# Cross attention with its queries, keys and values projected in three f16 products

## The reference

```python
x = x + self_attention(layernorm(layernorm(x)))        # 16 heads of 64, causal
x = x + cross_attention(layernorm(x), ctx)              # below
x = x + mixture_of_experts(layernorm(x))                # 8 experts, top 2, capacity

def cross_attention(x, context, w_qkv, w_proj, b_proj):  # 16 heads of 8, per batch
    q, k, v = split(x @ w_qkv.T)                         # 128 x 128 each
    k = concatenate([context_k, k])                      # 128 + 128 keys
    v = concatenate([context_v, v])
    attn = softmax(q * 8 ** -0.5 @ k.T)
    return (attn @ v) @ w_proj.T + b_proj
```

## Time and profile before

| | |
|---|---|
| median of 3 runs | 1158.15 us (1156.07 to 1158.4) |
| profiled execution | 1158.08 us, its span 1156.2 us |
| PE busy | 1074.3 us, 93% |
| DVE, ACT, POOL busy | 830.5, 674.7, 457.6 us |
| mean granted TensorE clock | 0.981 of full speed |
| self-attention alone | to about 435 us |
| cross attention, joined at first | about 439 to 866 us |
| expert weights and experts | about 866 us to the end |

### The profile page before, as it was taken

The page is one execution under the profiler, slowest core; times in us unless marked ns, Lnnn a source line. Parts: engine busy times, 40 slices in busy tenths (PEclk is TensorE's granted clock), DMA queues, the critical chain, the costliest instruction groups (busy, mean ns, idle before and its releaser), DMA issues.

```text
span 1156.2 us, 30982 instructions
## 1 busy us (share of the span) xinstructions
PE 1074.3 (93%) x12235; PEld 800.0 (69%) x12235; DVE 830.5 (72%) x1921; ACT 674.7 (58%) x1510; POOL 457.6 (40%) x799
## 2 busy tenths in 40 slices
PE   5999999999999998989999999999966999999997
PEld 4788888888888886667767677677643666565664
DVE  4776667776667774677777777777737788888887
ACT  2666666666656665555555565565534755555554
POOL 3444444444444444244344354453322522222222
PEclk9999999999999999899999999999976999999999
DMA  7000000000000000000000000002100000000000
GB/s 169 2 2 2 2 2 2 1 2 2 2 1 2 2 1 10 11 11 15 11 15 11 11 16 11 12 16 68 55 1 0 2 10 11 11 10 11 10 11 10
DMA packets 20658, 16.01 MB, mean 14 GB/s; under 512 B 7042, under 2 KB 18596, under 8 KB 20516
## 3 DMA queue, kind: packets, MB, share of 16 engines
q1 hardware_dynamic: 20176, 13.90, 4.6%
q10 hardware_dynamic: 340, 0.14, 0.1%
HBM read 11.94 MB, written 2.10 MB: 12 GB/s over the span
## 4 chain that ended last, share of the span: by engine, by line
PE 64%; issue 18%; DVE 8%; POOL 7%; ACT 2%; DMA 1%; SPq 0%; DVEq 0%; POOLq 0%
PE ps L971 56%; POOL h_lo L500 5%; PE ps L1022 5%; ACT q_shifted L572 2%; PE ps L1183 1%; DVE xT L677 1%; DMA wv<-in_L_attn_W_v 1%; DVE bst L852 1%; DVE x_all L848 1%; POOL probs L385 1%; PE ps L1213 1%; DVE padded L789 1%; DVE mv L855 1%; PE ps L1201 0%; PE ps L979 0%
## 5 line engine op out<-in xcount | busy, mean ns | idle before, releaser
L807 DVE TENSOR_REDUCE nmax<-ps 128x2 f32<-128x512 f32 x256 | 164.7, 686 | 15.4 <-PE ps L971 15.4
L597 ACT ACTIVATE probsT<-ps 128x512 f32<-128x512 f32 x256 | 139.7, 603 | 41.9 <-PE ps L971 41.0
L500 POOL TENSOR_TENSOR h_lo<-wk,h_hi 128x512 f16<-128x512 f32 x64 | 73.9, 1155 | 185.7 <-ACT h_hi L641 182.8
L535 ACT ACTIVATE probs<-ps,nmax 128x128 f32<-128x128 f32 x512 | 143.1, 384 | 6.9 <-DVE nmax L660 6.9
L529 ACT COPY probsT<-ps 128x512 f32<-128x512 f32 x128 | 75.2, 587 | 116.3 <-PE ps L1022 116.3
L385 POOL TENSOR_TENSOR probs<-probs,rinv 128x512 f32<-128x512 f32 x128 | 133.0, 1040 | 15.9 <-DVE rinv L670 15.9
L971 PE MATMUL ps<-probsT,va 128*32 128x128 f32 x2048 | 137.8, 277 | 0.0
L633 ACT ACTIVATE wq<-ps 128x512 f32<-128x512 f32 x128 | 76.6, 598 | 73.7 <-PE ps L971 73.6
L971 PEld LDWEIGHTS ps<-probsT,va 128*32 128x32 f32 x2048 | 103.0, 110 | 17.0 <-issue 6.7
L660 DVE TENSOR_REDUCE nmax<-ps 128x4 f32<-128x512 f32 x128 | 83.5, 673 | 38.9 <-PE ps L971 38.9
L955 DVE TENSOR_TENSOR h_lo<-wk,h_hi 128x512 f16<-128x512 f32 x64 | 71.8, 1122 | 43.8 <-ACT h_hi L641 43.8
(11 more groups left out here) (204 smaller groups left out, 2552.3 us busy)
## 6 DMA issues: line engine op xcount, KB each, us to landing
ctx_row<-in_ctx SPq DMA_DIRECT2D x32, 128.0 KB, 2.0
out_x<-x_all SPq DMA_DIRECT2D x8, 256.0 KB, 2.3
kT<-in_L_ffn_down_proj_w SPq DMA_DIRECT2D x1, 1024.0 KB, 10.8
wq<-in_L_attn_W_q SPq DMA_DIRECT2D x1, 512.0 KB, 5.0
wk<-in_L_attn_W_k SPq DMA_DIRECT2D x1, 512.0 KB, 8.8
wv<-in_L_attn_W_v SPq DMA_DIRECT2D x1, 512.0 KB, 10.4
wo<-in_L_attn_W_o SPq DMA_DIRECT2D x2, 256.0 KB, 6.7
x_all<-in_x SPq DMA_DIRECT2D x1, 256.0 KB, 3.0
```

Source lines behind the costliest of these rows:

```text
L500: nc.gpsimd.tensor_tensor(h_lo[:, e % 2, 0, :], hT[:, 0, :], h_hi[:, e % 2, 0, :], ALU.subtract).then_inc(hidden_low_first, 1)
L535: last = nc.scalar.activation(probs[:, u, i * P:(i + 1) * P], ps[u][:, i * P:(i + 1) * P], ACT.Exp, bias=nmax[:, u, i:i + 1])
L597: last = nc.scalar.activation(probsT[:, 2 * (t % 2) + a, :], ps[2 + a][:, :], ACT.Exp)
L807: last = nc.vector.reduce_max(nmax2[:, b % 2, t:t + 2, l + a], ps[a][:, :].rearrange("p (t k) -> p t k", t=2), AX_X, negate=True)
```

## The change

Cross attention's normalised input and its weights are split in two f16 parts each. The input's high part `xT2_hi` is written by ACT from the transpose's bank with a factor 16, and DVE makes the low part `xT2_lo` from the bank and the high part; both are kept in place of `xT2`. The weights are split once, in `prepare_cross`, with a factor 16 (`w2_hi`, `w2_lo`), and the threefold columns exist in both parts. Each f32 product is now three f16 products into the same place: high by high, low by high, high by low. The factor 256 that the banks then carry is taken out by the readers: `pack` multiplies the bank by 1/256 (a constant) and adds ACT's part, which ACT now makes with the mask as a scale (`q_sub`, `k_sub`); the copy of v has a constant scale.

```diff
+                    if g == 3 and valid(2):
+                        act.wait_ge(ca_xT_in_bank, b + 3)
+                        if valid(-2):
+                            act.wait_ge(ca_output, b - 1)
+                        nc.scalar.activation(xT2_hi[:, :], ps[7][:, 0:P], ACT.Copy, scale=X2_SCALE).then_inc(ca_xT_high, 1)
...
-                        dve.wait_ge(ca_xT_in_bank, n + 1)
-                        if valid(-2):
-                            dve.wait_ge(ca_output, b - 1)
-                        nc.vector.tensor_copy(xT2[:, :], ps[7][:, 0:P]).then_inc(ca_xT_taken, 1)
+                        dve.wait_ge(ca_xT_high, n + 1)
+                        nc.vector.scalar_tensor_tensor(out=xT2_lo[:, :], in0=ps[7][:, 0:P], scalar=X2_SCALE, in1=xT2_hi[:, :],
+                                                       op0=ALU.mult, op1=ALU.subtract).then_inc(ca_xT_taken, 1)
...
-                        nc.scalar.copy(q_hi[:, :, :], ps[5][:, :]).then_inc(ca_q_high, 1)
+                        nc.scalar.activation(q_sub[:, :, :], ps[5][:, :], ACT.Identity,
+                                             scale=low_q[:, 0:1]).then_inc(ca_q_subgh, 1)
...
-                        nc.scalar.activation(k_hi[:, :, :], ps[5][:, :], ACT.Identity,
-                                             bias=k_bias[:, 0:1]).then_inc(ca_k_high, 1)
+                        nc.scalar.activation(k_sub[:, :, :], ps[5][:, :], ACT.Identity, scale=low_k[:, 0:1],
+                                             bias=k_bias[:, 0:1]).then_inc(ca_k_subgh, 1)
...
-            def pack(dst, hi, bank, low):
-
-                return nc.vector.scalar_tensor_tensor(out=dst, in0=hi, scalar=low[:, :], in1=bank,
+            def pack(dst, part, bank):
+
+                return nc.vector.scalar_tensor_tensor(out=dst, in0=bank, scalar=1.0 / QKV_SCALE, in1=part,
                                                       op0=ALU.mult, op1=ALU.add)
...
+                        w_hi2, w_lo2 = (wqR_hi, wqR_lo) if g == 1 else (wkR_hi, wkR_lo)
                         for t in range(4):
-                            last = mm(ps[5][:, t * P:(t + 1) * P],
-                                      (wqR if g == 1 else wkR)[:, t, :, :, :].rearrange("p l a e -> p (l a e)"), xT2[:, :])
+                            for k, (w, xs) in enumerate(((w_hi2, xT2_hi), (w_hi2, xT2_lo), (w_lo2, xT2_hi))):
+                                last = mm(ps[5][:, t * P:(t + 1) * P], w[:, t, :, :, :].rearrange("p l a e -> p (l a e)"),
+                                          xs[:, :], k == 0, k == 2)
...
-                        mm(ps[6 if valid(0) else 4][:, 0:P], xT2[:, :], wqkvT[:, 2, :]).then_inc(ca_v_in_bank, 1)
+                        for k, (xs, w) in enumerate(((xT2_hi, w2_hi), (xT2_hi, w2_lo), (xT2_lo, w2_hi))):
+                            last = mm(ps[6 if valid(0) else 4][:, 0:P], xs[:, :], w[:, 2, :], k == 0, k == 2)
+                        last.then_inc(ca_v_in_bank, 1)
```

More of the change, by code:

```diff
@@ L36 @@
 SHIFT = 16.0
+X2_SCALE = 16.0
+W2_SCALE = 16.0
+QKV_SCALE = X2_SCALE * W2_SCALE
 KEYS2 = 2 * P
@@ L171, in build @@
         xT_lo = sb("xT_lo", [P, P], F16)
-        wqR = sb("wqR", [P, 4, 4, 4, E2])
-        wkR = sb("wkR", [P, 4, 4, 4, E2])
+        wqR_hi = sb("wqR_hi", [P, 4, 4, 4, E2], F16)
+        wqR_lo = sb("wqR_lo", [P, 4, 4, 4, E2], F16)
+        wkR_hi = sb("wkR_hi", [P, 4, 4, 4, E2], F16)
+        wkR_lo = sb("wkR_lo", [P, 4, 4, 4, E2], F16)
+        w2_hi = sb("w2_hi", [P, 3, P], F16)
+        w2_lo = sb("w2_lo", [P, 3, P], F16)
         k_bias = sb("k_bias", [P, 1])
         keys4 = sb("keys4", [P, H, 4, E2], F16)
-        q_hi = sb("q_hi", [P, 4, P], F16)
-        k_hi = sb("k_hi", [P, 4, P], F16)
+        q_sub = sb("q_sub", [P, 4, P], F16)
+        k_sub = sb("k_sub", [P, 4, P], F16)
         q_part = sb("q_part", [P, 2, 4, P], F16)
@@ L191, in build @@
         xn2 = sb("xn2", [P, D])
-        xT2 = sb("xT2", [P, P])
+        xT2_hi = sb("xT2_hi", [P, P], F16)
+        xT2_lo = sb("xT2_lo", [P, P], F16)
         xn3 = sb("xn3", [P, D])
@@ L601, in cross_attention @@
                         act.wait_ge(ca_v_in_bank, n + 1)
-                        nc.scalar.copy(va[:, n % 3, 1, :, 0:E2], ps[6 if valid(0) else 4][:, 0:P].rearrange(
-                            "p (h e) -> p h e", e=E2)).then_inc(ca_v_taken, 1)
+                        nc.scalar.activation(va[:, n % 3, 1, :, 0:E2], ps[6 if valid(0) else 4][:, 0:P].rearrange(
+                            "p (h e) -> p h e", e=E2), ACT.Copy, scale=1.0 / QKV_SCALE).then_inc(ca_v_taken, 1)
+                    if g == 3 and valid(2):
[3 more added lines that the diff above has]
+                        nc.scalar.activation(xT2_hi[:, :], ps[7][:, 0:P], ACT.Copy, scale=X2_SCALE).then_inc(ca_xT_high, 1)
             run_batches(act, -1, NB - 2, self_attention, range(G1))
@@ L767, in prepare_cross @@
                 dve.wait_ge(masks_ready, 1)
[L768 to L769 removed]
+                nc.vector.tensor_scalar(low_q[:, :], jmask[:, 2:3], -1.0 / QKV_SCALE, None, ALU.mult)
+                nc.vector.tensor_scalar(low_k[:, :], jmask[:, 1:2], -1.0 / QKV_SCALE, None, ALU.mult)
                 nc.vector.tensor_scalar(k_bias[:, :], jmask[:, 3:4], SHIFT, None, ALU.mult).then_inc(masks_ready, 1)
@@ L794, in cross_attention @@
                         n = b + 1
-                        dve.wait_ge(ca_q_high, n + 1)
-                        pack(q_part[:, n % 2, :, :], q_hi[:, :, :], quads, low_q).then_inc(ca_q_packed, 1)
+                        dve.wait_ge(ca_q_subgh, n + 1)
+                        pack(q_part[:, n % 2, :, :], q_sub[:, :, :], quads).then_inc(ca_q_packed, 1)
                     if g == 3 and valid(1):
                         n = b + 1
-                        dve.wait_ge(ca_k_high, n + 1)
-                        pack(kT2[:, n % 3, :, P:KEYS2], k_hi[:, :, :], quads, low_k).then_inc(ca_k_packed, 1)
+                        dve.wait_ge(ca_k_subgh, n + 1)
+                        pack(kT2[:, n % 3, :, P:KEYS2], k_sub[:, :, :], quads).then_inc(ca_k_packed, 1)
                     if valid(0):
@@ L985, in self_attention @@
                             pe.wait_ge(raw_s_taken, 3)
-                            pe.wait_ge(quad_weights_ready, 10)
+                            pe.wait_ge(quad_weights_ready, 20)
                             pe.wait_ge(bo_ready, 1)
```

25 lines of the change are left out of this document (17 added, 8 removed).

## The result

The changed kernel takes **1149.3 us** (median of four runs, 1147.88 to 1150.16), the kernel before in the same comparison 1158.2 (1156.07 to 1158.4). The ratio is 0.9926, with a 95% interval of 0.9909 to 0.9943: faster by 0.7%, or 8.9 us, where 16 were forecast. The profiled execution has a time of 1149.91 and a span of 1148.2 us, so the two spans, 1156.2 and 1148.2, differ by 8.0. The chain of waits still closes every period in the same way, with ScalarE's high part as one link more. The helper that issues matmuls is now line 993 and the padded write line 812.

A forecast was written before the change was run, and what follows sets the result against it. PE work with two hand-overs was taken to bound each period. Full periods -14.6, b = 30 -0.75, b = 0 and 1 -2.0, start +1.0: -16.3 from 1158.1, thus 1142 us; forecast 1136 to 1150, with rival 2 to 1156.

The forecast's parts named there:

- rival 2: Only part of the gain, through a few clock falls, one lost cover or slower f16 products: 1150 to 1156, chance 0.20.
- the hop: After the output product, DVE waits for ACT's high part: 0.28 us lost per period, from 0.23 to 0.30.
- hidden q product: PE's query product gains 0.40 us, worth nothing because ACT's first exponentials release the second scores 3.29 us into the period.
- main term: Shorter k and v products on PE: together 0.80 us off each full period, bounds 0.62 and 0.84.
- Rival 4: The q product counts too, if ACT's exponentials come earlier than read: 28 x 0.35 less, 1132 us, chance 0.05.
- Rival 3: Nothing measurable: the wait through ACT after the output product costs 0.6 us, not 0.28; 1156 to 1160.5, chance 0.07.
- Cadence and covers: f16 products run 0.056 us each; q_sub and k_sub take 0.10 more each, hidden, and q_part is ready for k.
- rival 1: PE's idle places in the loop lie close, so the clock falls: slower, 1184 us with one fall per period, chance 0.09.
- the borders of the k and v products: Changeovers between scores and f16 products on PE: 0.07 us saved ahead of k and of v, 0.01 added behind each.
- b = 0 and 1: First two periods, PE at half clock with the q product on the path: -2.0 us, bounds -1.2 and -2.8.
- Start: DVE's weight preparation grows by 2.4 us, partly taken up by idle time: +1.0 us, bounds +0.4 and +1.8.
- b = 30: The period where nothing is transposed any more, so ACT's high part adds no wait: -0.75 us.

The follow-up runs named there:

- the f32 kernel with the two moves: Kernel before, in f32, with VectorE's xT copy put after the next period's first maxima and the context's keys ahead of the shift: 1151.42 us.
- residual first: Changed kernel with VectorE adding the residual straight after the output product, the high part after it, the low part after the next first maxima: 1134.07 us.
- the last three kernels: Changed kernel with residual first and v product behind k: 1131.93 us; also k packed earlier: 1128.38; also keys' transposes ahead of the shift on PE: 1128.87.
- v beside k: Changed kernel with the v product moved up to stand right behind the k product, no longer between 32-row scores: 1143.65 us.
- keys ahead: Changed kernel with the context's keys transposed on PE ahead of the shift and cast by ACT before q_shifted: 1144.6 us.

## Why the prediction was right or wrong

The change made the kernel faster and the time, 1149.3, lies in the range, at the edge between the main forecast (1136 to 1150) and rival 2. None of rival 2's causes came about. The net gain per full period was 0.18 us and not 0.52, so the direction, the hop and the hidden q product were right, and the size of the main term was not. That the time still fell under 1150 is in part luck, as the sum on the spans below shows.

**Right.**
- *The q gain is worth nothing.* The q product takes 0.68 us (506.65 to 507.33), and the second scores wait 0.22 for the exponentials and start 3.27 us into the period; before it was 3.29. Cutting the product to a third changed nothing. Rival 4 is out.
- *The hop.* The forecast was 0.28 us lost, the trace shows 0.41 - 0.10 = 0.31. ACT was free in time, idle for 0.28 before it. Rival 3, a hop of 0.6, is out. That ACT itself is the cause was not right: on DVE alone the second step costs as much.
- *Cadence and covers.* From 509.92 to 510.54 there are 11 steps of 0.056. ACT's q_sub and k_sub take 0.72 and 0.78, some 0.1 more each as priced, and no wait for the third or fourth exponentials appeared.
- *The clock in the loop.* 1.00 from 480 to 820 with idle times of 0.74, 0.46 and 0.22 in a period, so rival 1 didn't occur. The last period with a shift even began with a hole of 0.50, like the 0.51 of the earlier trace rows, and the clock stayed at 1.00 from 842 to 848. So it did in the traces of all eleven other kernels, in ten of them after a hole of 0.50 or 0.51 and in the f32 kernel with the two moves after a longer one:

```profile
839.67 0.23 PE L974 MATMUL ps<-ident_h,padded 128*128 128x128 f16 x1 [0.86 <-DVE padded L794]
```

```profile
842.00:848.00 6.00, 5.38 (x85) 4.06 (x85) 1.33 (x6) 3.75 (x8) 0.72 (x2) 1.00 0.01 3
```

The fall of the earlier trace rows stands in one trace of thirteen. The reading that such a hole makes the clock fall was too much read into one case.

**The step that failed: the borders of the k and v products.** The forecast took 0.07 us off *ahead* of each, since "scores are followed by an f16 product after 0.25 us (839.85 to 840.10)", and put 0.01 *behind* each. But that row is one group of 32-row products behind another. A full f16 product follows scores after 0.33 us (509.59 to 509.92) and 0.32 (512.50 to 512.82), just as the f32 one did. Behind it the scores came 0.77 us after the start of k (509.92 to 510.69), which is 12 x 0.056 and 0.10 more, and 0.27 after the start of v (512.82 to 513.09), 0.17 and 0.10 more. So k gained 1.10 - 0.77 = 0.33 and not 0.50, and v 0.42 - 0.27 = 0.15 and not 0.32. Together that is 0.48 in place of 0.80, below the lower bound of 0.62, because the bound too kept the 0.07. The moved v product shows the same from the other side, 0.20 us for one pair of borders. A net of 0.48 - 0.31 = 0.17 is what these rows give, and the periods show 0.18. Two of the signs named ahead told of it: periods of 12.04 and not 11.7, and 0.77 and not 0.67 from k to the next scores.

The page's figure, some 81 ns per product (the Trainium skill, "TensorE: Matmul & The Clock Gate", Back-to-back issue gap), would by the forecast's estimate have given a gain of about 0.4 and 1152 us, nearer than mine. It comes near by chance: products here are 56 ns apart, and what is missing lies at the borders.

**Terms of the wrong size.**
- *b = 0 and 1:* forecast -2.0, measured about 0 (the shift of b = 2 starts at 481.13, before at 481.01, and after was 0.17 behind already at 459 us; b = 2 itself gained 0.16). The clock at which it was priced was not the same: it was granted 0.57 and 0.74 between 460 and 480, against 0.64 and 0.85. The shorter products were run for longer at 1.2 GHz. As an estimate, 20 us at a mean of 0.655 in place of 0.745 hold 1.8 us of full clock less, which is about the whole term.
- *Start:* forecast +1.0, measured +0.5: from the preparation's first copy to the first maxima it takes 4.97 us in place of 4.46. The work up to the bias grew by 1.7 and not 2.4: four f16 copies with their memset took 0.38 (25.13 to 25.51) in place of 0.55. The idle 0.26 and 0.87 us of the earlier trace rows took it up as forecast. That the maxima start only 0.05 later by the clock of the trace is chance: the preparation itself began 0.46 sooner, and that beginning lies anywhere from 22.03 to 23.51 us in the kernels traced here.
- *b = 30:* -0.5, forecast -0.75.
- *Not in the sum:* three longer periods that went (-0.9), and -1.8 behind the last shift: it starts 6.2 us sooner (839.20 against 845.44), the span is 8.0 shorter. Both vary between traces whatever the products. A period longer by 0.27 to 0.38 us stands once in residual first and once in each of the last three kernels, and in v beside k there is none. From the last shift to the end it is 310.8 us before and 309.0 after, but 309.6 in the f32 kernel with the two moves and 308.5 to 310.0 in the ten others. Before is the only one with the fall of the clock there.

Together on the spans: 27 periods -4.9, b = 2 -0.2, b = 30 -0.5, the start +0.5 and b = 0 and 1 +0.1 make -4.9; the sooner beginning -0.5, the longer periods -0.9 and the end -1.8 make -3.1 more, thus -8.0. So some 5 us are shown to come from the change, and 3 stand in places that vary from trace to trace. The medians moved by 8.9; as only one execution of each kernel was profiled, how much of this lies in such places is not shown. With the 5 us alone the time would be 1153, in rival 2's part of the range.

Four small slips stand in the forecast's numbers. With nothing behind k and v their gain is at most 0.82, not 0.84; the hop's lower bound is 0.23 - 0.05 = 0.18, not 0.17; the best case per period is then 0.64, not 0.67. And twice 0.056 is 0.112, not 0.107. None changes the account.

**What the products are worth where the split is off the chain.** The kernel before with residual first and keys ahead has periods of 11.97 us, the changed kernel with the residual first 11.47. That is 0.50, close to the 0.48 that k and v gained on PE, and more than twice the 0.18 that the change gave with the split on the chain. The two kernels also differ in where the keys stand, which alone gave the changed kernel 0.28, so it is an estimate.

## What to carry to other kernels

Price a product with its borders: how long its predecessor and successor take to change over depends on what kinds stand side by side, and a row between two other kinds is no price for it. When a copy on the closing chain is split in two, first ask whether the step that follows it needs the copy at all; moving it behind the residual was worth three times the whole change in the loop (0.57 against 0.18 us per period). And a move that fills a hole pays only if the thing waited for comes earlier too: list the waits after each move, since twice here the gain turned up there under another name.

## What the runs showed of the hardware that I had not expected

- One visit of full 128-row f16 products among 32-row ones costs 0.20 us beyond the products: 0.32 to 0.33 against 0.22 on the way in, 0.10 on the way out.
- On VectorE a 128x128 step that depends on the one before it starts 0.33 us behind it, an independent one 0.21; where ScalarE makes the first of the two it is 0.31.
- Where the loop begins at the lower clock, kernels that differ in the order of a few instructions got the full clock back at different times: between 470 and 480 us the granted clock was 0.87, 0.74, 0.52 or 0.51. What sets it stays open, and with one profiled execution of each kernel it may be chance.
- A hole of 0.50 to 0.51 us on TensorE, with two waits for ScalarE behind it, left the clock at full speed in eleven traces and was followed by a fall in one.
